# Attention scores of a small vision tower on one core, computed in blocks of 64 tokens by four heads

## The reference

```python
B, T, E = x.shape          # T is 16 tokens, 8 heads of D = 16
gammas = 1.0 - 2.0 ** (-5.0 - jnp.arange(H, dtype=jnp.float32))
q = (x @ wq.T + bq).reshape(B, T, H, D)
k = (x @ wk.T + bk).reshape(B, T, H, D)
v = (x @ wv.T + bv).reshape(B, T, H, D)
rel = idx[None, :] - idx[:, None]
decay = jnp.where(rel[None] >= 0, gammas[:, None, None] ** rel[None], 0.0)
scores = jnp.einsum('bihd,bjhd->bhij', q, k) / math.sqrt(D) * decay[None]
out = jnp.einsum('bhij,bjhd->bihd', scores, v).reshape(B, T, E)
return jax.nn.silu(x @ wg.T + bg) * out
```

## Time and profile before

| | |
|---|---|
| median of 3 runs | 279.29 us |
| the runs | 278.91, 279.29, 289.74 us |
| span of the profiled execution | 277.0 us |
| busy: PE, PEld | 188.9, 138.3 us |
| busy: DVE, ACT, POOL | 154.0, 79.1, 127.1 us |
| share of the chain that ended last: PE, POOL, DVE | 30%, 22%, 17% |

### The profile page before, as it was taken

One profiled execution on the slowest core, in us unless ns is written; L12 is line 12 of the kernel. 1 busy time (PEld: TensorE's weight loads), 2 busy tenths in 40 slices (PEclk: granted clock), 3 DMA queues, 4 the chain that ended last, 5 costly groups with the idle time before them and its releaser, 6 DMA issues.

```text
span 277.0 us, 3884 instructions
## 1 busy us (share of the span) xinstructions
PE 188.9 (68%) x1048; PEld 138.3 (50%) x1048; DVE 154.0 (56%) x568; ACT 79.1 (29%) x209; POOL 127.1 (46%) x214
## 2 busy tenths in 40 slices
PE   0888999988999888889796412997999972000000
PEld 0234577755665567667575302996999851000000
DVE  2433658767787779888786586354236541311311
ACT  0034644444332545443340000443334410000000
POOL 3013333366565566755655466033122007777770
PEclk9999999999999999999995555799579997555555
DMA  7999999999000000000000005498889451232231
GB/s 270 348 381 377 415 389 424 386 346 205 29 19 12 19 19 20 12 19 14 30 19 19 21 30 164 112 287 270 254 251 289 151 164 46 69 93 68 66 94 29
DMA packets 35596, 43.12 MB, mean 156 GB/s; under 512 B 3120, under 2 KB 29808, under 8 KB 34288
## 3 DMA queue, kind: packets, MB, share of 16 engines
q1 hardware_dynamic: 32560, 35.47, 39.1%
q0 software_dynamic: 3008, 7.34, 8.7%
HBM read 24.71 MB, written 18.09 MB: 155 GB/s over the span
## 4 chain that ended last, share of the span: by engine, by line
PE 30%; POOL 22%; DVE 17%; issue 14%; DMA 12%; SPq 2%; POOLq 1%; ACT 0%; DVEq 0%
POOL X L1024 9%; DMA xb<-expert_rows 6%; PE bank L554 6%; POOL rs L967 5%; PE bank L563 5%; DMA R<-rows 4%; POOL expert_rows L985 4%; PE bank L546 4%; PE bank L439 3%; PE bank L427 3%; PE bank L391 3%; POOL ve L966 2%; DVE mpos L794 2%; DVE xrow L834 2%; DVE pos L798 1%
## 5 line engine op out<-in xcount | busy, mean ns | idle before, releaser
L1024 POOL DMA_INDIRECT X<-expert_rows,slots x32 | 32.0, 1000 | 23.1 <-DMA expert_rows<-ys 13.7
L985 POOL DMA_INDIRECT expert_rows<-xrow,slots x32 | 34.0, 1063 | 11.4 <-issue 7.4
L966 POOL TENSOR_SCALAR ve<-mv 128x1 f32<-128x1 f32 x48 | 9.1, 189 | 64.8 <-DVE mv L744 32.3
L439 PEld LDWEIGHTS bank<-vg,ST 128*128 128x128 f32 x256 | 33.8, 200 | 3.5 <-issue 2.8
L439 PE MATMUL bank<-vg,ST 128*128 128x16 f32 x256 | 32.3, 260 | 0.0
L391 PE MATMUL bank<-X,W 128*128 128x512 f32 x48 | 26.4, 651 | 8.4 <-DVE W L709 6.6
L427 PE MATMUL bank<-qm,kT 128*128 128x512 f32 x64 | 30.8, 604 | 0.0
L621 ACT ACTIVATE qm<-bank,bqm,C 128x128 f32<-128x128 f32 x64 | 24.1, 457 | 21.9 <-PE bank L415 20.8
L967 POOL TENSOR_TENSOR rs<-ve,mhalf 128x1 f32<-128x1 f32 x48 | 26.8, 557 | 4.0
L903 DVE TENSOR_TENSOR hT<-bank,gs 64x512 f32<-64x512 f32 x17 | 11.8, 694 | 28.7 <-ACT gs L678 28.7
L937 DVE SCALAR_TENSOR_TENSOR h<-X,pw,h 128x128 f32<-128x128 f32 x32 | 9.9, 352 | 32.0 <-DMA X<-expert_rows,slots 31.7
(11 more groups left out here) (110 smaller groups left out, 332.6 us busy)
## 6 DMA issues: line engine op xcount, KB each, us to landing
expert_rows<-fill SPq DMA_DIRECT2D x10, 1024.0 KB, 22.3
X<-xp SPq DMA_DIRECT2D x12, 512.0 KB, 15.4
w13s<-w SPq DMA_DIRECT2D x16, 256.0 KB, 4.5
xb<-expert_rows SPq DMA_DIRECT2D x16, 256.0 KB, 5.0
expert_rows<-ys POOLq DMA_DIRECT2D x12, 256.0 KB, 4.6
w2s<-w SPq DMA_DIRECT2D x16, 128.0 KB, 5.6
WP<-wp SPq DMA_DIRECT2D x3, 640.0 KB, 6.4
XE<-xe SPq DMA_DIRECT2D x4, 384.0 KB, 17.4
```

The source lines that it names most:

```text
L439: mm = nc.tensor.matmul(O[:, hh * HD:(hh + 1) * HD], ST[:, t % 2, hh], vg[:, t % 4, hh * HD:(hh + 1) * HD], start=True, stop=True)
L966: own(pool.tensor_scalar(ve[:, t % 2], mv[:, t % 2, 1:2], 1.0, eps, ALU.mult, ALU.add))
L985: pool.indirect_dma_start(buf, bass.IndirectOffsetOnAxis(ap=slots[:, k, t:t + 1], axis=0), xrow[:, t % XR], None, bounds_check=NE * CAP - ...
L1024: pool.indirect_dma_start(pr[:, t, k], None, buf, bass.IndirectOffsetOnAxis(ap=slots[:, k, t:t + 1], axis=0), bounds_check=NE * CAP - 1, o ...
```

## The change

The zeroed second buffer of `kT` goes, and the keys are evacuated by one full-height ACT operation. The scores of a tile are four matmuls: for each block `c` of 64 tokens and each half `n` of four heads one with 64 rows (the half's features), 64 weight columns (the block's keys) and 4 x 64 moving columns (the block's queries under the four masks). The output of block `c` lies on partitions 64c to 64c + 63, of half `n` in the bank `S[:, n]`. The two banks are now one tensor `S`, in the place of `S0` and `S1`. VectorE multiplies block by block: operation `c` reads 64 partitions of both banks, 2 x 4 x 64 elements each, and writes the diagonal block of all eight heads of `ST`. The blocks off the diagonal are never written; GpSimd zeroes both buffers of `ST` once at the start. Both halves of `attend` wait for both operations.

```diff
-        kT = sb("kT", [P, 2, 2, P])
+        kT = sb("kT", [P, 2, P])
-        bank = [ctx.enter_context(nc.psum_tensor(f"bank{n}", [P, 512], F32)) for n in range(8)]
+        bank = [ctx.enter_context(nc.psum_tensor(f"bank{n}", [P, 512], F32)) for n in range(5)]
+        S = ctx.enter_context(nc.psum_tensor("scores", [P, 2, 512], F32))
+        bank += [S[:, 0], S[:, 1], ctx.enter_context(nc.psum_tensor("bank7", [P, 512], F32))]
@@ scores, TensorE (TB = 64, NTB = 2)
                 if t >= 1:
-                    pe.wait_ge(st_ready, 2 * t)
-                for n, s in enumerate((S0, S1)):
-                    mm = nc.tensor.matmul(s[:, :], kT[:, t % 2, n], qm[:, t % 2].rearrange("p a i -> p (a i)"),
-                                          start=True, stop=True)
+                    pe.wait_ge(st_ready, NTB * t)
+                for c in range(NTB):
+                    for n in range(2):
+                        rows, toks = slice(n * P // 2, (n + 1) * P // 2), slice(c * TB, (c + 1) * TB)
+                        mm = nc.tensor.matmul(S[toks, n, 0:QM * TB], kT[rows, t % 2, toks], qm[rows, t % 2, :, toks],
+                                              start=True, stop=True)
@@ attend, TensorE
-                pe.wait_ge(st_ready, 2 * t + n + 1)
+                pe.wait_ge(st_ready, NTB * (t + 1))
@@ evac_qk, ACT
-                    act.wait_ge(kT_zeroed, 1)
-                for n in range(2):
-                    own = slice(n * P // 2, (n + 1) * P // 2)
-                    ins = nc.scalar.activation(kT[own, t % 2, n], QK[own, P:2 * P], ACT.Identity, bias=bk[own])
-                ins.then_inc(qk_ready, 1)
+                nc.scalar.activation(kT[:, t % 2], QK[:, P:2 * P], ACT.Identity, bias=bk).then_inc(qk_ready, 1)
@@ decay_scores, VectorE
+                    dve.wait_ge(ST_zeroed, 1)
-                for n, s in enumerate((S0, S1)):
+                for c in range(NTB):
+                    toks = slice(c * TB, (c + 1) * TB)
                     nc.vector.tensor_tensor(
-                        ST[:, t % 2, n * QM:(n + 1) * QM].rearrange("p a i -> p (a i)"), s[:, :],
-                        decay[:, n * 512:(n + 1) * 512], ALU.mult).then_inc(st_ready, 1)
+                        ST[toks, t % 2, :, toks].rearrange("p (n m) i -> p n m i", m=QM),
+                        S[toks, :, 0:QM * TB].rearrange("p n (m i) -> p n m i", m=QM),
+                        decay[toks].rearrange("p (n m i) -> p n m i", n=2, m=QM)[:, :, :, toks],
+                        ALU.mult).then_inc(st_ready, 1)
@@ GpSimd's start
-            pool.memset(kT[:, :, :, :], 0.0).then_inc(kT_zeroed, 1)
             pool.memset(fill[:, :, :], 0.0).then_inc(filled_tile, 1)
+            pool.memset(ST[:, :, :, :], 0.0).then_inc(ST_zeroed, 1)
```

More of the change, by code:

```diff
@@ L52 @@
 QM = 4
+TB = 64
+NTB = P // TB
 NE = 64
@@ L209, in tower @@
         spare_filled = sem("spare_filled")
-        ones_set, kT_zeroed = sem("ones_set"), sem("kT_zeroed")
+        ones_set, ST_zeroed = sem("ones_set"), sem("ST_zeroed")
         w_ready, wd_in_ready, wd_ps, wd_ready, cvec_ready, bqm_ready, before_ready = (sem(n) for n in (
```

## The result

| | before | changed kernel |
|---|---|---|
| first measurement, runs | 278.91 to 289.74 us, median 280.4 (4 runs) | 283.49 to 284.63 us, median 284.19 (4 runs) |
| beside the last experiments | 276.65 to 283.78 us, median 278.95 (23 runs) | 279.72 to 297.89 us, median 286.58 (14 runs) |
| ratio, first and second measurement | | 1.0167 (1.0100 to 1.0234) and 1.0111 (1.0062 to 1.0160) |
| span of the profiled execution | 277.0 us | 282.8 us |

The changed kernel is slower, by 1.1 to 1.7% in the ratio (changed over before) and by 3.8 and 7.6 us in the medians of the two measurements. The ratio leaves out runs more than 1.5% above a kernel's fastest, nine of the changed kernel's 14 in the second measurement and three of before's 23; so medians over all runs and their range stand beside it from here on. The forecast was 279.7 us, 277.6 to 282.8, with no change that can be told.

What follows compares the result with a forecast made beforehand. Bound: TensorE early in the token loop, VectorE and GpSimd in the middle, mostly VectorE's ST operation late. Early -0.6, middle 0, late +1.04 gave +0.4 us: 279.7 us against 279.29, range 277.6 to 282.8.

Steps and rivals of the forecast that it cites:

- the last rival: Token loop: lighter TensorE load lets the granted clock fall to 1.2 GHz mid-loop, 286 us; chance 0.05.
- The price of a fall: Token loop: one iteration at the lower clock grows from 7.4 us of TensorE work to about 14.8, +6.7 us over 8.1.
- My milder form: End of the token loop: the clock falls one or two us earlier than at 146 us, costing 1 us.
- A call of the scores: Score matmuls of one tile on TensorE: 1.47 us forecast against 1.72 before, 0.25 us less, including 0.39 for shape changes.
- lower bound: Score matmuls of a tile: all four blocks side by side, 2 x 0.215 + 0.39 = 0.82 us, 0.90 less than before.
- The full-overlap rival: Score matmuls: all four blocks side by side, 0.82 us a call; total -0.1 us, 279.2 us; chance 0.20.
- my middle value: Score matmuls: a block's second pass runs beside the next block's first, 5 steps of 0.215 us, 1.47 us with shape changes.
- early stretch: Token loop, 27 to 52 us, TensorE setting the pace: forecast 0.6 us gained, with VectorE becoming the bound.
- VectorE's late start: ST operations: starting at partition 64 between operations starting at 0 costs 0.13 us before and behind, +0.26 us a tile.
- late stretch: Late token loop, chain through VectorE's ST operation: four iterations at +0.26 us each, +1.04 us.
- middle stretch: Token loop, 52 to 103 us, chain through VectorE and GpSimd, period 8.1 us: forecast change 0.
- ACT: Evacuation of kT: one full-height operation of about 0.36 us replaces a pair of 0.74, 0.38 us less; value 0.

Runs made afterwards that it cites:

- the last experiments: Four kernels beside the kernel before: changed again, 286.58 us; changed plus two thrown-away matmuls, 284.81; before plus one, 277.41; one VectorE operation a tile plus two, 274.62.
- VectorE's part alone: The kernel before with only the two VectorE operations by blocks, TensorE and ACT as before: 280.45 us, ratio 1.0058.
- one-operation kernel: The changed kernel with only diagonal blocks in ST and decay, one VectorE operation a tile, attend by blocks: 278.32 us, ratio 0.9941 against the kernel before.
- the filler: A thrown-away full-shape matmul of 0.86 us for tiles 4 and later, here added to the one-operation kernel: 273.75 us, ratio 0.9755 against the kernel before.
- blocks three times: The changed kernel with its four block matmuls issued three times over, 24 passes instead of 8 a tile: 279.55 us, ratio 1.0038 against the kernel before.

## Why the prediction was wrong

**The step that failed** is the chance and the argument of the last rival, that the clock falls inside the loop. It was named, with its mechanism, and given 0.05, on the argument that "the lightest parts of a period, attends and waits, hold no scores". The first fall of the changed kernel is at 65 us. The four microseconds ahead of it hold the scores, then a short wait and the 16-column passes of attend with the projections between them:

```profile
61.16 0.66 PE L433 MATMUL scores<-qm,kT 64*64 64x256 f32 x8
62.24 0.33 PE L470 MATMUL bank<-C,xrow 128*128 128x128 f32 x1 [0.42 <-DVE xrow L836]
62.41 0.97 PE L445 MATMUL bank<-vg,ST 128*128 128x16 f32 x8
63.23 0.47 PE L418 MATMUL bank<-xnT,SQ 128*128 128x128 f32 x2
```

The score passes lie directly beside the light part. Shortening them from 1.72 to 0.61 us lets the stretch with little work begin a microsecond earlier in every period. My argument cut the period into parts and compared them one by one. That it is this stretch which brings the fall is argued, not shown: no run moved the scores away from it. What the runs show is that less TensorE work in a period brings falls and more of it takes most of them away. I had also read the 289.74 us run of before as scatter. It left no profile, so whether it was the clock, and in which stage, stays open.

**The price of a fall** was mis-sized as well: one whole iteration at the lower clock, +6.7 us. A fall may cover part of a period, and TensorE has slack: the periods with a dip in them took 8.3 to 9.5 us in the first profile (11.0 at most in the second), where 8.2 are normal. So not one fall made the loss but five, at 65, 85, 99, 123 and 137 us, the last of which never ended within the loop: 9.5 and 9.1 us for two iterations that took 6.6 and 6.3 (5.65 of the 8.7 us lost behind `i` = 6). My milder form, the fall at the end coming one or two us earlier for 1 us, was this one, only that it came some 10 us earlier, at 137 instead of 146.5.

**A call of the scores**: taken at 1.47 us, measured 0.61, below even the lower bound of 0.82, since the changes of shape cost 0.19 us together and not 0.39. The full-overlap rival, to which I gave 0.20, was the right one; and the trace agrees with what the Trainium skill (TensorE: Matmul & The Clock Gate, Part 3) says, that matmuls on different row groups run concurrently: two steps of 0.215 us for eight passes, where my middle value had five. For the time of the early stretch it made no difference, and for the clock it made it worse: the better the packing works, the lighter the load.

**The early stretch**: right. `go` at `i` = 5 forecast 0.31 us earlier, measured 0.43; after `mpos`, at `i` = 6, forecast 0.6, measured 0.62. VectorE became the bound there, with `go` to `go` of 6.78 and 6.87 us against the forecast 6.75 and 6.97.

**VectorE's late start**: right where it was seen (the pair 1.39 us, its second operation 0.69 us behind the first where 0.72 was forecast, the next PSUM reader 1.42 us behind the first), wrong in what it costs. The late stretch was charged 1.04 us; over three of its four iterations it cost 0.13. The chain there was VectorE's by a hair: in the same iterations GpSimd's send and `rs` lead to the same `go`, and with VectorE's part alone the chain changes over to them in two of the three. In turn the middle stretch, put at 0, costs 0.1 us a period through the held `vg`. The total of the two, +1.2 us for VectorE's part alone, is near what was forecast, by luck.

**ACT**: one evacuation of 0.38 us for two, without effect, as forecast. The expert stage moved with the loop's end, apart from its own share of the lower clock.

## What to carry to other kernels

Where TensorE is not the bound but lies close behind it, its granted clock is part of the schedule: taking a microsecond of its work out of an 8 us period made the kernel slower by 1 to 3%, and putting useless work back took that loss away. It also made the one-operation kernel faster, and, by 0.7% and by a path that isn't shown, the kernel before. Look at the granted clock of each stretch after every change that relieves TensorE, look at the spread of many runs, and keep a throw-away matmul at hand in a place where TensorE waits. The relief is worth having only together with something that shortens the engines that set the pace: here one VectorE operation a tile instead of two, with the filler, 1.6 to 2.5% under the kernel before, from four runs of each version (ratio 0.9755, 0.9658 to 0.9851).

## What the runs showed of the hardware

- Blocks of 64 rows by 64 columns in float32 run side by side: eight passes of 256 columns take 0.42 us more when added to a call (blocks three times), as two passes in turn; 0.19 us are left for entering and leaving the shape.
- The granted clock fell to 1.2 GHz with TensorE marked busy 78% of a period (6.61 of 8.50 us) in the period ahead of the second fall, and with no wait of TensorE over 1.2 us between 50 and 150 us, in either profile of the changed kernel. The Trainium skill (TensorE: Matmul & The Clock Gate, HAM oscillation) tells of a kernel in which waits for transfers bring such falls again and again; in this loop TensorE waited for no transfer, only for VectorE.
- An operation of VectorE that reads PSUM from partition 0 is held behind its neighbour (0.38 instead of 0.25 us from start to start) when the last PSUM reader, two operations back, began at partition 64.
- Matmuls from two row halves of the array can write the two partition halves of one PSUM bank directly one after the other: attend by blocks does so in every tile, 16 passes in 0.53 us (33.48 to 34.01 in the one-operation kernel), where eight full-height passes took 0.82 (63.73 to 64.55 before). Whether two of them are ever in flight together isn't shown.
